# Attention and expert layer: the next block's scores ahead of the shift, expert chunks behind it, and the second expert product in three rounded terms

## What is computed

```python
x = x + attention(layernorm(x))   # 16 heads of 8; every query block of 64 attends
                                  # to its own key block and to one chosen block
def ffn(x, w1, b1, w2, b2, wr, br):
    logits = x @ wr + br
    topk_vals, topk_idx = jax.lax.top_k(logits, 2)          # 2 of 4 experts
    gates = softmax(topk_vals)
    h = gelu(einsum('nd,edh->enh', x, w1) + b1[:, None, :]) # 4 experts, 512 hidden
    y = einsum('enh,ehd->end', h, w2) + b2[:, None, :]
    ...                                                     # less constants of each expert
    out = einsum('nk,nkd->nd', gates, chosen y)
x = x + ffn(layernorm(x), ...)
```

## Time and profile before

| | |
|---|---|
| median of three runs | 1009.64 us (1007.39 to 1009.81) |
| the profiled execution | 1008.49 us, of which its span 1006.9 us |
| granted TensorE clock, mean | 0.948 of full speed |
| busy over the span | PE 932.7 us (93%), DVE 552.1 (55%), ACT 460.2 (46%), POOL 172.6 (17%) |
| c_down, L386 | 260.8 us busy |
| scores, L295 | 138.2 us busy |
| c_up, L247 to L249 | 314.6 us busy |

### The profile page before, as it was taken

One profiled execution on the slowest core, in us unless ns is written; L12 is line 12 of the kernel. 1 busy time (PEld: TensorE's weight loads), 2 busy tenths in 40 slices (PEclk: granted clock), 3 DMA queues, 4 the chain that ended last, 5 costly groups with the idle time before them and its releaser, 6 DMA issues.

```text
span 1006.9 us, 24099 instructions
## 1 busy us (share of the span) xinstructions
PE 932.7 (93%) x9572; PEld 599.8 (60%) x9572; DVE 552.1 (55%) x1555; ACT 460.2 (46%) x740; POOL 172.6 (17%) x174
## 2 busy tenths in 40 slices
PE   3584889999999999999999999999999999999996
PEld 2362666575666666565666556566666656665652
DVE  6262645747475655747474565746575665734321
ACT  1131345363735445373635436363645436363641
POOL 3120101121212121120212121111212121110221
PEclk8575679999999999999999999999999999999998
DMA  7424052342506243352515344251615334250110
GB/s 208 115 70 120 4 142 88 109 135 72 164 14 177 63 138 103 96 147 61 164 26 150 88 123 119 76 168 36 176 38 140 99 114 119 74 159 2 54 51 14
DMA packets 96819, 101.06 MB, mean 100 GB/s; under 512 B 8744, under 2 KB 83376, under 8 KB 96688
## 3 DMA queue, kind: packets, MB, share of 16 engines
q1 hardware_dynamic: 94400, 86.89, 30.9%
q0 software_dynamic: 2304, 12.58, 3.9%
HBM read 48.98 MB, written 29.49 MB: 78 GB/s over the span
## 4 chain that ended last, share of the span: by engine, by line
PE 67%; DVE 17%; issue 6%; ACT 4%; SPq 3%; DMA 2%; POOL 0%; POOLq 0%; DVEq 0%
PE y_ps L386 15%; PE s_ps L295 10%; PE s_ps L318 6%; DVE rmax L609 6%; PE o_ps L329 5%; PE s_ps L247 5%; PE s_ps L249 5%; PE s_ps L248 5%; ACT hid L883 4%; SPq L1032 3%; PE v_ps L304 2%; DVE gate_cols L705 2%; PE o_ps L336 2%; PE a_ps L256 2%; PE a_ps L359 1%
## 5 line engine op out<-in xcount | busy, mean ns | idle before, releaser
L386 PE MATMUL y_ps<-hid,w2s 128*128 128x512 f32 x480 | 260.8, 629 | 0.8 <-DVE yT L705 0.2
L609 DVE TRANSPOSE_TENSOR_REDUCE rmax<-s_ps 128x16 bf16<-128x512 f32 x256 | 167.8, 693 | 165.6 <-PE s_ps L295 165.6
L847 ACT ACTIVATE prob<-s_ps 128x1024 f32<-128x1024 f32 x128 | 131.2, 1025 | 201.0 <-PE s_ps L318 200.8
L883 ACT ACTIVATE hid<-s_ps,b1s 128x512 f32<-128x512 f32 x256 | 171.5, 688 | 37.1 <-PE s_ps L249 35.4
L295 PE MATMUL s_ps<-qdiag,kv 64*128 64x512 f32 x768 | 138.2, 467 | 19.2 <-DMA kv<-kv_chosen 18.2
L840 ACT COPY vaug<-v_ps 128x128 f32<-128x128 f32 x128 | 34.0, 265 | 205.6 <-PE v_ps L304 205.6
L318 PEld LDWEIGHTS s_ps<-nmax,hone 16*128 16x128 bf16 x2048 | 69.7, 95 | 97.6 <-DVE nmax L618 96.6
L247 PE MATMUL s_ps<-xnhi,w1hi 128*128 128x512 f32 x256 | 112.2, 438 | 1.4
L967 POOL TENSOR_TENSOR yT<-yT,gate_cols 128x512 f32<-128x512 f32 x48 | 61.4, 1279 | 283.2 <-DVE gate_cols L705 282.8
L295 PEld LDWEIGHTS s_ps<-qdiag,kv 64*128 64x128 f32 x768 | 86.6, 256 | 35.2 <-issue 27.4
L248 PE MATMUL s_ps<-xnlo,w1hi 128*128 128x512 f32 x256 | 101.2, 395 | 0.0
(11 more groups left out here) (139 smaller groups left out, 1079.1 us busy)
## 6 DMA issues: line engine op xcount, KB each, us to landing
gate_cols<-gates SPq DMA_DIRECT2D x64, 256.0 KB, 5.2
kv_table<-stage SPq DMA_DIRECT2D x16, 768.0 KB, 3.9
kv<-stage SPq DMA_DIRECT2D x16, 768.0 KB, 6.2
kv_chosen<-selected SPq DMA_DIRECT2D x16, 768.0 KB, 5.3
kv<-kv_chosen SPq DMA_DIRECT2D x16, 768.0 KB, 4.9
qdiag<-qpair SPq DMA_DIRECT2D x512, 16.0 KB
xs<-in_x SPq DMA_DIRECT2D x16, 256.0 KB, 4.5
out_x<-x SPq DMA_DIRECT2D x16, 256.0 KB, 4.6
```

The lines of the kernel that those rows point to most:

```text
L386: ins = pe.matmul(dst[:], w2s[:, n, :], hid[:, n, :], start=(c == 0), stop=(c == C - 1))
L609: v.tensor_reduce(rmax[m % 2][:, half * 8:(half + 1) * 8, :], s_ps[m % 2][:, half * N:(half + 1) * N].rearrange("p (a c) -> p a c", c=32), ...
L847: act.activation(prob[m % 2][:].rearrange("p h s -> p (h s)"), s_ps[m % 2][:], ACT.Exp, scale=SCALE).then_inc(exped, 1)
L883: act.activation(hid[:, k, :], up_ps[up_bank(k)], ACT.Gelu, bias=b1s[:, k:k + 1]).then_inc(gelued, 1)
```

## The change

Four things change together.

1. In the step, `scores(b, m + 1)` now stands in front of `shift(b, m)` instead of behind it. Where b is 2 or more, both `c_down` of a step stand behind the shift, but for steps 0 and 7, which keep their first one in front.
2. `c_down` is three matmuls of float32r operands: high part of w2 by high part of hid, low by high, and high by low. w2 is split once (GpSimd, batch 0). hid is split chunk by chunk: the high part (a rounded copy) on ScalarE, `c_hi`, the low part (the difference) on GpSimd, `c_lo`; the first two chunks of a batch are copied on GpSimd. There are two pairs of buffers, so that a high part waits for the matmuls of two chunks earlier. At the end, behind the loop, GpSimd copies and VectorE subtracts, with eight pairs of buffers.
3. VectorE's `a_select(b + 1)` moves from the front of step 6, before `block_max`, to its end, before `c_gates_turned`. GpSimd's `a_select` stands behind the two `c_lo` of step 6.
4. The buffers for the gates are 2 instead of 4, and SyncE reads two of the four gates in the next batch.

```diff
@@ tensor, loop
                     row_max(b, m)
...
-                    if b >= 2:
+                    edge = m in (0, M - 1)
+                    if b >= 2 and edge:
                         c_down(b - 2, 2 * m)
+                    if m + 1 < M:
+                        scores(b, m + 1)
                     shift(b, m)
...
-                    if m + 1 < M:
-                        scores(b, m + 1)
                     if m in (4, 6):
                         o_project(b, (m - 4) // 2)
+                    if b >= 2 and not edge:
+                        c_down(b - 2, 2 * m)
                     if m in (2, 4, 6):
                         o_rows(b, (m - 2) // 2)
@@ tensor, c_down
-                pe.wait_ge(gelued, UPS * b + n + 1)
-                ins = pe.matmul(dst[:], w2s[:, n, :], hid[:, n, :], start=(c == 0), stop=(c == C - 1))
+                pe.wait_ge(*low_of(b, n))
+                pe.matmul(dst[:], w2hi[:, n, :], hi, start=(c == 0), stop=False)
+                pe.matmul(dst[:], w2lo[:, n, :], hi, start=False, stop=False)
+                ins = pe.matmul(dst[:], w2hi[:, n, :], lo, start=False, stop=(c == C - 1))
@@ vector, loop
-                        if m == 6:
-                            tied = a_select(b + 1)
...
                     if b >= 1 and m == 5:
                         c_split(b - 1)
+                    if b + 1 < B and m == 6:
+                        tied = a_select(b + 1)
                     if b >= 1 and m == 6:
                         c_gates_turned(b - 1)
@@ vector, behind the loop
+            def c_los(b, first, last):
+                for n in range(first, last):
+                    c_lo(b, n)
...
@@ scalar
+            def c_hi(b, n):
+                hi, _, was = parts_of(b, n)
+                act.wait_ge(*weighed_of(was))
+                act.copy(hi, hid[:, n, :]).then_inc(hi_cast, 1)
...
                     shift_exp(b, m)
                     if b >= 1 and m == 0:
                         c_columns(b - 1)
+                    if b >= 2 and m + 1 < M:
+                        c_hi(b - 2, 2 * m + 2)
                     if m in (3, 5, 7):
                         o_columns(b, (m - 3) // 2)
...
+                    if b >= 2 and m + 1 < M:
+                        c_hi(b - 2, 2 * m + 3)
@@ gpsimd
+            def c_lo(b, n):
+                hi, lo, _ = parts_of(b, n)
+                g.wait_ge(*high_of(b, n))
+                g.tensor_tensor(lo, hid[:, n, :], hi.bitcast(F32), ALU.subtract).then_inc(lo_pooled, 1)
...
+                    if b >= 2 and m + 1 < M:
+                        c_lo(b - 2, 2 * m + 2)
                     if b >= 1 and m == 5:
                         c_split(b - 1)
-                    if b >= 2 and m in (4, 6):
-                        c_sum(b - 2, m // 2 - 1)
+                    if b >= 2 and m + 1 < M:
+                        c_lo(b - 2, 2 * m + 3)
+                    if b + 1 < B and m == 6:
+                        a_select(b + 1)
                 if b >= 2:
                     c_sum(b - 2, E - 1)
+                if b >= 1:
+                    for n in range(NH):
+                        c_hi(b - 1, n)
+                    for n in range(NH):
+                        c_lo(b - 1, n)
@@ sync, loop
                 if b >= 3:
                     store(b - 3)
+                if b >= 2:
+                    take_gate(b - 2, 2)
                 if b + 1 < B:
                     place_q(b + 1, 0, range(8))
+                if b >= 2:
+                    take_gate(b - 2, 3)
```

More of the change, by code:

```diff
@@ L150, in layer @@
         gate_cols = [sb(f"gate_cols{i}", [P, N]) for i in range(NG)]
+        hidhi, hidlo = ([sb(f"hid{part}{i}", [P, N], F32R) for i in range(NH)] for part in ("hi", "lo"))
         yT = sb("yT", [P, N])
@@ L243, in bank_of, with parts_of, high_of, low_of @@
             return next(of for of, _ in banks.values() if use in of.at)
+        TAIL, NT = UPS * (B - 2) + 2, 8
+        def parts_of(b, n):
+            at = UPS * b + n
+            if at < TAIL:
+                return hidhi[at % NH][:], hidlo[at % NH][:], at - NH
+            i = (at - TAIL) % NT
+            hi, lo = (q[:, i // 4, i % 4 * 2:i % 4 * 2 + 2, :].rearrange("p h s -> p (h s)") for q in qdiag)
+            return hi, lo, at - NT if at - NT >= TAIL else None
+        def high_of(b, n):
+            at = UPS * b + n
+            if at >= TAIL:
+                return hi_moved, NH * (B - 1) + at - TAIL + 1
+            return (hi_moved, NH * b + n + 1) if n < NH else (hi_cast, (UPS - NH) * b + n - NH + 1)
+        def low_of(b, n):
+            at = UPS * b + n
+            return (lo_done, at - TAIL + 1) if at >= TAIL else (lo_pooled, at + 1)
+        def weighed_of(at):
+            b, n = divmod(at, UPS)
+            if n % C == C - 1:
+                of = bank_of("down", b, n // C)
+                return of.full, of.at["down", b, n // C]
+            return weighed, at - at // C + 1
+        SPLIT_W1, SPLIT_W2 = E, 2 * E
         def tensor(pe):
@@ L977, in pool @@
                 for m in range(M):
+                    if b >= 2 and m in (4, 6):
+                        c_sum(b - 2, m // 2 - 1)
                     if b + 1 < B:
@@ L1099, in sync @@
                 if b >= 1:
-                    for e in range(E - 1):
-                        take_gate(b - 1, e)
+                    take_gate(b - 1, 0)
                 if b + 1 < B:
@@ L1104, in sync @@
                 if b >= 1:
-                    take_gate(b - 1, E - 1)
+                    take_gate(b - 1, 1)
             b = B - 1
             store(b - 2)
+            take_gate(b - 1, 2)
+            take_gate(b - 1, 3)
             put_gates(b)
-            for e in range(E):
-                take_gate(b, e)
+            take_gate(b, 0)
+            take_gate(b, 1)
             store(b - 1)
+            take_gate(b, 2)
+            take_gate(b, 3)
             store(b)
@@ L1213, in general_tensor @@
                     for c in range(C):
[L1214 to L1215 removed]
+                        rows = hid[:, e * C + c, k * P:(k + 1) * P]
+                        pe.matmul(y_ps[:, k * P:(k + 1) * P], rows, w2hi[:, e * C + c, :].bitcast(F32), start=(c == 0), stop=False)
+                        ins = pe.matmul(y_ps[:, k * P:(k + 1) * P], rows, w2lo[:, e * C + c, :].bitcast(F32),
+                                        start=False, stop=(c == C - 1))
                 ins.then_inc(turn, 1)
```

87 lines of the change are left out of this document (62 added, 25 removed).

## The result

The changed kernel takes 1057.21 us (median of 4 runs, 1055.86 to 1061.49), the kernel before 1008.51 in the same series: a ratio of 1.0496, 95% interval 1.0454 to 1.0538. It is 5% slower. Its profiled execution took 1055.86 us, its span 1054.1, 47.2 longer than before.

A forecast was written before the change was run, and what follows sets the result against it. TensorE (93% busy) was taken as the bound, the chosen block's path only 0.65 us shorter. Thirteen batches +31, batch 0 +3.5, batch 1 +1, batch 15 -3.5, tail -1: +31 on 1008.5, 1041 as median; range 1006 to 1070.

The forecast's parts named there:

- Cheaper downs: On TensorE, a down takes 0.77 us instead of 0.96; with 256 downs 43.5 us of its work go.
- Steps 0 to 6: In a steady batch, these six steps take 31.3 us, 1.8 less; bounds 33.1 and 29.3.
- The addition for the held gate multiplication: In step 3, VectorE's gate multiplication falls beside a low part on GpSimd: 0.4 us.
- Step 6 and the block: Late choice: index at 6.25, gather 6.5, block at 23.4 us; step 6 to begin 3.5 longer; bounds 22.4 and 23.9.
- The two holds: In step 6, GpSimd holds two of VectorE's choice instructions; one already counted, the second adds up to 0.9 us.
- Rival (a): In step 6, no second hold on VectorE: gather at 5.7, batch 58.1, total 1025 us; chance 0.20.
- (c): The chosen block's path behind the gather shortens to 14 us, no second hold: batch 55.5, total 989; chance 0.14.
- The clock: Rival: TensorE's clock falls in front of begin, some 2.5 us a batch, total 1073; chance 0.10.
- Start: Batches 0 and 1: later index costs +3.5 us in batch 0, and +1 in batch 1, which has some slack.
- Batch 15: The last batch makes no choice and keeps most of its saving: -3.5 us.
- Tail: Behind the loop, 32 downs are 5 us shorter but need copy and subtraction chains: -1, between -5 and +5.
- (d): Rounded chunks take as long as before, low parts late for their downs: batch 2 us more, 1065; chance 0.05.

The follow-up runs named there:

- e8: Changed kernel with the choice back in its old place on both queues, GpSimd's xnlo and sum of step 6 moved behind gather and low parts: 993.5 us, ratio 0.9847.
- e6: Changed kernel without the splits of hid, downs reading constant tiles (other output), choice still late: 1018.4 us, ratio 1.0108.
- e13: Changed kernel with useless matmuls filling TensorE's idle stretches ahead of the shift of step 7 and ahead of begin: 1046.9 us, ratio 1.0384.
- e5: Kernel before with only the next scores issued ahead of the shift: 997.7 us, ratio 0.9881.
- e9: Changed kernel with SyncE's read of the chosen blocks issued right behind their write: 1034.1 us, ratio 1.0258.
- e2: Kernel before with only VectorE's choice moved late, to the end of step 6: 1065.0 us, ratio 1.0577.
- e3: Changed kernel with VectorE's choice back early, GpSimd's gather still behind the low parts of step 6: 1069.6 us, ratio 1.0644.

## Why the prediction was right or wrong

1041 was forecast, with a range of 1006 to 1070, and slower with a chance of 0.77. The sign, the mechanism and the place were right; the size was 16 us short. By its steps:

**Cheaper downs: right.** 0.77 forecast, 0.79 and 0.81 measured. TensorE's busy time fell by 23.5 and not by 40: with the same matmuls e8 has 886.2, 46.5 less than before. The missing 23 go with the clock, whose mean was 0.922 in the changed kernel and 0.946 in e8: matmuls took longer at the lower level.

**Steps 0 to 6: 31.3 forecast, 30.7 measured.** Each step came within 0.2 but the one from 3 to 4, put at 5.75, which took 5.45. The addition for the held gate multiplication, 0.4, didn't reach the path. e6, with 29.65, shows that the splits still held back 1.0 of what TensorE could do, close to the lower bound of 29.3.

**Step 6 and the block: right.** Index 6.25 forecast, 6.09 measured; gather 6.5 and 6.4; block path behind it 16.9 and 17.1 (5.31, 6.71, 5.14); step 6 to begin 23.4 and 23.5. The two holds came, though not on the instruction I named: L636 took 0.25, since it started 0.17 before the sum on GpSimd ended; L639 and L641, beside the low parts, took 0.64 and 1.13. Which of a row of small instructions is held is a matter of tenths; that some are isn't. Rival (a), no second hold, fell with that, and (c) too: the block's path behind the gather kept its three lengths to 0.3 us, SyncE's stretch to 0.01.

**The clock: the step that failed.** The prediction put the fall of the clock into a rival, as all or nothing, with 0.10, and argued against it from a single idle of 2.28 us in the tail. In fact it is a term of the sum: over batches 2 to 14 begin to S0 took 5.48 in the mean, not the 4.74 of an upper clock, which is 9.6 us in thirteen batches. With this term the sum's batch comes to 2.4 + 0.7 = 3.1, against 37.9 / 13 = 2.9 measured. e13 shows that the idle is its cause. So the forecast's slower batches came out nearly right in part by luck: steps 0 to 6 took 0.5 less than forecast (30.8 in the mean), and the clock took 0.7 more.

**The ends.** Start: +4.5 forecast, +2.3 measured. Batch 15: -3.5 forecast, -1.1 measured, in part since its own begin met the lower clock (6.10 instead of 4.74). **Tail: -1 forecast, with bounds of 5 on either side; +8.2 measured.** This term was mis-sized beyond its bounds. The 5 us for cheaper downs came (67.6 before, 62.9 in e6), but the splits, put at 4, cost 12.9. The chain was named (a copy on GpSimd and a subtraction on VectorE for each down), but the same hold that made the choice late was not applied to it: four subtractions take 2.48 us where nothing holds them and up to 4.75 beside GpSimd's casts, and thirty such subtractions stand ahead of downs. How much of the 12.9 is the hold stays open, as said above.

Against the forecast that makes: thirteen batches +6.9 (clock +9.6, steps 0 to 6 about -6 by their mean of 30.8, the rest of begin to S0 and of step 6 to begin +3), the tail +9.2, batch 15 +2.4, start -2.2. That is 16.3, the distance from 31 to 47.2.

**(d) fell** (a down isn't held by its low part but once in a batch, for 0.40). That the scores ahead of the shift cost nothing was right, but e5 shows that they gain 11 us; the prediction gave them nothing.

## What to carry to other kernels

A chain that leaves the core (index, gather, write, read) and returns to the critical engine has a due time: before anything is put ahead of its first instruction, on either queue, compare its slack (0.65 us here) with what that costs. Keep GpSimd's long two-operand instructions away from a row of small VectorE instructions that somebody waits for: shifting two of them by a few places was worth 30 us here, more than half of what the splits cost in that order. And an idle stretch ahead of dense matmuls has a second price, the clock behind it, which belongs into the sum for a share of the batches and not into a rival; here that share was between half of them (changed kernel) and nearly all (e6).

## What the hardware showed unexpectedly

Two short waits on TensorE, 0.40 and 1.26 us with a down of 0.8 between them, were enough for the granted clock to fall to 0.55 to 0.60 in the next 3 us, in ten of thirteen batches of the changed kernel and in all of e9; five useless matmuls with zero weights in that place kept it at 1.00. Behind the begins of batches 2 to 15, with a wait of 0.4 to 3.4 us ahead of each, it fell in seven of fourteen, those with the six longest waits among them. In e2, e3 and e6, where nearly all of these waits are 1.4 to 3.6 us, it fell in twelve, twelve and thirteen of fourteen. The length of the wait alone doesn't decide: in e2 the clock stayed up behind one of 2.28 and fell behind one of 1.37.

VectorE's cast of xnhi, with one operand in SBUF, is held by GpSimd too: 0.90 beside a low part, 0.42 in e6, where no low part runs. The hold works in both directions: GpSimd's cast of 128x512 takes 0.61 alone and 0.84 in the mean in the tail, where VectorE subtracts beside it.
